# Which engine makes the low parts of tiles 10, 12, 16 and 18 of a split-precision mixture-of-experts kernel

## The reference

```python
x = x + 0.5 * ffn(layernorm(x), ...)      # B, T, D = 8, 512, 128
x = x + attn(layernorm(x), ...)           # two 128x128 projections, gates
x = x + 0.5 * ffn(layernorm(x), ...)

def ffn(x, centroids, expert_biases, Ws_up, Ws_down, W_up, W_down):   # E = F = 64, TOP_K = 8
    shared = silu(xf @ Ws_up) @ Ws_down
    aff = xf @ centroids.T
    _, idx = top_k(aff + expert_biases, TOP_K)
    w = sigmoid(take_along_axis(aff, idx))
    w = w / (sum(w) + 1e-08)
    cw = zeros((T, E)).at[arange(T)[:, None], idx].add(w)
    h = silu(einsum('td,edf->etf', xf, W_up))
    y = einsum('etf,efd->etd', h, W_down)
    return shared + einsum('etd,te->td', y, cw)
```

## Time and profile before

| what | value |
|---|---|
| median of 3 runs | 836.47 us (836.36 to 836.81) |
| profiled execution, span from first to last instruction | 834.9 us |
| PE / DVE / ACT / POOL busy | 809.7 / 698.6 / 654.2 / 404.6 us |
| granted PE clock | full (2.4 GHz level) in all slices |
| length of a body A phase / a body B phase | 50.3 / 51.6 us |

### The profile page before, as it was taken

How to read it: one execution, slowest core, us unless ns; L and a number is a source line. 1 busy time by engine, 2 the same in 40 slices (tenths; PEclk the granted TensorE clock), 3 DMA queues, 4 the chain that set the end, 5 groups by cost and what they waited for, 6 DMA issues and landing times.

```text
span 834.9 us, 12478 instructions
## 1 busy us (share of the span) xinstructions
PE 809.7 (97%) x3691; PEld 648.0 (78%) x3691; DVE 698.6 (84%) x1456; ACT 654.2 (78%) x1204; POOL 404.6 (48%) x355
## 2 busy tenths in 40 slices
PE   7899999999999999999999999999999999999998
PEld 5777778877778777787777877778778787788786
DVE  7998888798887988879888798787896987888875
ACT  5886679778787787877878788786878868876975
POOL 2764545544445444554545455354453644544443
PEclk9999999999999999999999999999999999999999
DMA  7000000000000000000000000000000000000000
GB/s 264 20 1 26 1 1 1 1 13 14 13 1 1 25 0 13 0 0 25 0 13 0 0 25 0 13 0 0 25 0 0 0 0 27 0 1 1 14 0 13
DMA packets 16046, 11.51 MB, mean 14 GB/s; under 512 B 1680, under 2 KB 14992, under 8 KB 16016
## 3 DMA queue, kind: packets, MB, share of 16 engines
q1 hardware_dynamic: 16016, 11.15, 4.2%
HBM read 9.05 MB, written 2.10 MB: 13 GB/s over the span
## 4 chain that ended last, share of the span: by engine, by line
PE 47%; DVE 18%; issue 15%; POOL 11%; ACT 7%; DMA 0%; POOLq 0%; DVEq 0%; ACTq 0%
POOL g_lo L351 8%; PE up L700 7%; PE up L701 7%; PE up L702 7%; PE y_ps L700 7%; PE y_ps L702 7%; PE y_ps L701 7%; DVE g_lo L578 3%; DVE up L569 3%; DVE gated L569 3%; DVE normed L515 2%; PE side L709 2%; ACT up L410 2%; ACT g_hi L418 2%; POOL rstd L341 2%
## 5 line engine op out<-in xcount | busy, mean ns | idle before, releaser
L351 POOL TENSOR_TENSOR g_lo<-gated,g_hi 128x512 fp32r<-128x512 f32 x256 | 332.3, 1298 | 370.9 <-ACT g_hi L418 370.3
L410 ACT ACTIVATE up<-up 128x512 f32<-128x512 f32 x528 | 310.9, 590 | 74.7 <-PE up L702 73.3
L569 DVE TENSOR_TENSOR gated<-up,cw 128x512 f32<-128x512 f32 x256 | 174.7, 682 | 51.6 <-ACT up L410 47.7
L569 DVE TENSOR_TENSOR up<-up,cw 128x512 f32<-128x512 f32 x256 | 175.9, 687 | 48.8 <-ACT up L410 45.5
L700 PE MATMUL up<-x_hi,wu_hi 128*128 128x512 f32 x512 | 204.3, 399 | 7.2 <-DVE g_lo L578 7.2
L700 PE MATMUL y_ps<-g_hi,wd_hi 128*128 128x512 f32 x512 | 208.4, 407 | 1.7 <-POOL g_lo L351 1.7
L702 PE MATMUL y_ps<-g_hi,wd_lo 128*128 128x512 f32 x512 | 202.4, 395 | 0.0
L701 PE MATMUL up<-x_lo,wu_hi 128*128 128x512 f32 x512 | 202.2, 395 | 0.0
L702 PE MATMUL up<-x_hi,wu_lo 128*128 128x512 f32 x512 | 201.9, 394 | 0.0
L701 PE MATMUL y_ps<-g_lo,wd_hi 128*128 128x512 f32 x512 | 201.8, 394 | 0.0
L418 ACT CAST g_hi<-gated 128x512 fp32r<-128x512 f32 x256 | 157.7, 616 | 48.1 <-DVE gated L569 45.8
(11 more groups left out here) (100 smaller groups left out, 564.1 us busy)
## 6 DMA issues: line engine op xcount, KB each, us to landing
x_in<-in_x SPq DMA_DIRECT2D x8, 256.0 KB, 2.7
wu_raw<-in_w_up SPq DMA_DIRECT2D x4, 512.0 KB, 5.8
wd_raw<-in_w_down SPq DMA_DIRECT2D x4, 512.0 KB, 6.8
x_res<-in_x SPq DMA_DIRECT2D x8, 256.0 KB, 2.7
out<-out_sb SPq DMA_DIRECT2D x7, 256.0 KB, 2.2
out<-out_sb SPq DMA_DIRECT2D x2, 128.0 KB, 1.8
sm_raw<-in_ident SPq DMA_DIRECT2D x2, 64.0 KB, 5.2
ident<-in_ident SPq DMA_DIRECT2D x1, 64.0 KB, 2.6
```

The costliest lines, as they stand in the source:

```text
L351: nc.gpsimd.tensor_tensor(g_lo[:, i, :], gated[:, t // 2 % ORING, :], g_hi[:, i, :].bitcast(fp32), ALU.subtract).then_inc(lo_done[1], 1)
L410: nc.scalar.activation(up[i][:, :], up[i][:, :], ACT.Silu).then_inc(silu_done, 1)
L569: nc.vector.tensor_tensor(gated[:, t // 2 % ORING, :] if t % 2 else up[i][:, :], up[i][:, :], cw[ph.q][:, :], ALU.mult).then_inc(gate_done, 1)
```

## The change

The split of the low parts between DVE and POOL by odd and even is replaced by two lists, `POOL_TILES` (the odd tiles and 10, 12, 16, 18) and `VECTOR_TILES` (the rest). `OWN[t]` says which list a tile is in, `RANK[t]` its place in it. All counts, buffers and waits that used `t % 2` and `t // 2` use them. For the four tiles the gate writes to `gated`, ACT's high part and POOL's low part read from there, and `free_bank` waits for the gate. The ring `gated` has five buffers in place of four. POOL has 20 low parts per phase (16 before), DVE 13 (17).

```diff
--- before.py
+++ after.py
@@ -17,8 +17,13 @@
 SLOTS = -(-NT // RING) * RING
 LAG = RING + 1
 GRING = LAG + 1
-ORING = 4
-NLOW = (NT // 2 + 1, NT // 2)
+
+POOL_TILES = sorted({t for t in range(NT) if t % 2} | {10, 12, 16, 18})
+VECTOR_TILES = [t for t in range(NT) if t not in POOL_TILES]
+OWN = [int(t in POOL_TILES) for t in range(NT)]
+RANK = [(VECTOR_TILES, POOL_TILES)[OWN[t]].index(t) for t in range(NT)]
+ORING = 5
+NLOW = (len(VECTOR_TILES), len(POOL_TILES))
 AW = D + 2
 AS = 256
 NPIECE = 4
@@ -239,7 +244,7 @@
         def low_count(ph, t):
 
             back, t = before(t)
-            return NLOW[t % 2] * (ph.p - back) + t // 2 + 1
+            return NLOW[OWN[t]] * (ph.p - back) + RANK[t] + 1
 
         def halves(ph, name, t):
 
@@ -348,7 +353,7 @@
 
                 i = t % GRING
                 pool.wait_ge(hi_done, NT * ph.p + t + 1)
-                nc.gpsimd.tensor_tensor(g_lo[:, i, :], gated[:, t // 2 % ORING, :], g_hi[:, i, :].bitcast(fp32),
+                nc.gpsimd.tensor_tensor(g_lo[:, i, :], gated[:, RANK[t] % ORING, :], g_hi[:, i, :].bitcast(fp32),
                                         ALU.subtract).then_inc(lo_done[1], 1)
 
             def split_up(i):
@@ -360,7 +365,7 @@
 
             def phase(ph):
                 for t in range(SLOTS):
-                    if (t - 1) % 2 and 0 < t <= NT:
+                    if 0 < t <= NT and OWN[t - 1]:
                         low_part(ph, t - 1)
                     if t in ph.at.get("wu_lo", ()):
                         split_up(ph.at["wu_lo"].index(t))
@@ -414,7 +419,7 @@
                     act.wait_ge(gate_done, NJ * ph.p + t)
                 else:
                     act.wait_ge(silu_done, NT * ph.p + t + 1)
-                src = gated[:, t // 2 % ORING, :] if t % 2 else up[t % RING][:, :]
+                src = gated[:, RANK[t] % ORING, :] if OWN[t] else up[t % RING][:, :]
                 nc.scalar.copy(g_hi[:, t % GRING, :], src).then_inc(hi_done, 1)
 
             def y_copy(p):
@@ -566,7 +571,7 @@
 
                 i = t % RING
                 dve.wait_ge(silu_done, NT * ph.p + t + 1)
-                nc.vector.tensor_tensor(gated[:, t // 2 % ORING, :] if t % 2 else up[i][:, :], up[i][:, :], cw[ph.q][:, :],
+                nc.vector.tensor_tensor(gated[:, RANK[t] % ORING, :] if OWN[t] else up[i][:, :], up[i][:, :], cw[ph.q][:, :],
                                         ALU.mult).then_inc(gate_done, 1)
 
             def low_part(ph, t):
@@ -601,7 +606,7 @@
                         dve.wait_ge(cw_done[ph.q], ph.use + 1)
                     if 0 < t < NT:
                         gate(ph, t)
-                    if t % 2 and 1 < t <= NT:
+                    if 1 < t <= NT and not OWN[t - 1]:
                         low_part(ph, t - 1)
                     if t in ph.at.get("wd_lo", ()):
                         split_low(wd_lo, wd_raw, wd_hi, ph.at["wd_lo"].index(t), wd_hi_done, wd_lo_done)
@@ -753,7 +758,7 @@
 
             def down_product(ph, t):
                 made, t = low_count(ph, t), before(t)[1]
-                pe.wait_ge(lo_done[t % 2], made)
+                pe.wait_ge(lo_done[OWN[t]], made)
                 i = t % GRING
                 if t > 0:
                     last = split_product(y_ps[:, :], (wd_hi[:, t - 1, :], wd_lo[:, t - 1, :]), (g_hi[:, i, :], g_lo[:, i, :]),
@@ -767,7 +772,7 @@
             def free_bank(ph, t):
 
                 back, tile = before(t)
-                if tile % 2:
+                if OWN[tile]:
                     pe.wait_ge(gate_done, NJ * (ph.p - back) + tile)
                 else:
                     pe.wait_ge(lo_done[0], low_count(ph, t))
```

## The result

The changed kernel takes 847.3 us (median of 4 runs, 847.12 to 847.64) against 836.57 of the kernel before beside it: a ratio of 1.0128, with a 95% interval of 1.0114 to 1.0143. The forecast was 848 us. The profiled execution has a span of 845.3 us, 10.4 more than before. Of all the executions timed for this document one, of `after_x2_psum`, ran at a lower granted clock (0.851) and took 883.8 us; it is left out.

The account below looks back on a forecast made before the run. PE, busy 97% of the span, was taken as the bound, so only holes in its matmul train count. 7.8 (body B, phase 2) + 1.2 (body A) + 2.4 (phases 1, 14) = 11.4 us, giving 848 us; range 833 to 853.

Parts of the forecast that it names:

- Holes removed: PE's idle gaps at tile 10 (body B) and tile 16 (body A) go: -0.66 us in each steady phase.
- Blocks queue behind POOL's operations: With POOL operations back to back, each normed block on DVE waits for one; body B's four take 5.1 us, before 1.4.
- Body B, +1.3: Five phases B and phase 2: new 1.95 us hole at PE's transpose of normed, one of 0.66 gone; 7.8 us in all.
- Body A, +0.2: Six phases: tile 17's down product waits for POOL, a hole of 0.85 us for one of 0.66; 1.2 us in all.
- Phases 1 and 14, +1.2 each: Four x2 blocks wait behind POOL's low parts; between -0.7 and +1.9 us each, taken as +1.2, 2.4 us in all.
- The sum: All phases together: 11.4 us more on the profiled execution, a span of 846.3 us.
- rival 1: The gain comes through, normed done before PE asks: -2.8 us, 833.7; chance 0.16.
- Rival 2: Low 17 waits for its high part, blocks three or four fall into that gap, body B about 0: 839 us; chance 0.20.
- rival 3: DVE blocks hold POOL in turn, down products wait too: +1 us in 12 phases, 857 to 860 us; chance 0.11.
- rival 4: Nothing moves, holes closed and opened cancel: 835 to 838 us; chance 0.07.

Follow-up runs that it names:

- after_x2_psum: The changed kernel with DVE's four x2 blocks in phases 1 and 14 reading their first operand from PSUM (wrong values): 843.23 us, 1.0076 of before.
- low_10: The changed kernel with only tile 10 added to POOL's odd tiles, not 12, 16 and 18: 833.89 us, 0.9970 of the kernel before.
- after_norm_psum: The changed kernel with DVE's normed blocks from x1 read from PSUM instead of SBUF (wrong values): 835.12 us, 0.9980 of the kernel before.
- u_t_later: The changed kernel with PE's transpose of normed and its copy two slots later in body B and phase 2: 847.46 us, 1.0131 of before.

## Why the prediction was right, step by step

- **Holes removed** (-0.66 in each steady phase). Right for both: neither the hole at tile 10 nor that at tile 16 is in the trace of after, and low_10 shows the 0.66 of body B alone, to the hundredth.
- **Blocks queue behind POOL's operations.** Right, and the main term. The pairs take 2.56 and 2.46 us; worked out were 2.5 and 2.5. after_norm_psum takes this one thing away, and the total falls below that of the kernel before. Two slips around it changed nothing in the sum: POOL is not "busy without a break", since the prediction's own clock has low 17 start 1.4 us after low 16 ends, as it does in the trace; and the four blocks took 1.57 us before, not 1.4, and 5.02 now, not 5.1.
- **Body B, +1.3.** Measured +1.39 each, phase 2 +1.44. The new hole is 1.96 us long (2.19 from the start of the matmul before it, less the pace of 0.23), as worked out. On phase 6's clock low 15 was put at 349.7 (it is 349.60), the end of the blocks at 356.3 (356.14), the transpose at 356.4 (356.29). Six of them were 7.8 us in the sum and are 8.4. What I said of the transpose as the place where PE waits is true, but u_t_later shows that it is not what the hole depends on.
- **Body A, +0.2.** The mechanism was right, the sign of the sum was not. The down product of tile 17 has its hole, of 1.06 us rather than 0.85: lows 15 and 16 take 2.74 us together, not 2.55. DVE's `biased`, which has both operands in SBUF, runs from 305.86 to 307.11, across the change from the one to the other; that it holds low 16 up is inferred from that. But I had only looked at the hole of tile 16, and two small ones of body A went as well: the transpose of `w_dup` at 318.55 and the first up product of the next phase at 322.71, some 0.3 and 0.2 us in the kernel before. So body A is 0.16 shorter, phase 13 0.63: -1.4 in the sum in place of +1.2.
- **Phases 1 and 14, +1.2 each.** They are +2.19 and +1.37, 3.6 us in place of 2.4. The term was mis-sized. It stood between bounds of -0.7 and +1.9, nearer the upper one, with no row for phase 14, and none for the 1.1 us of four unhindered `x2` blocks (after_x2_psum has them at 1.12). The `x2` blocks took 4.24 us (3.9 worked out), and after_x2_psum shows that they carry phase 14's loss and some two thirds of phase 1's. The rest of phase 1 is a cost that the prediction has nowhere: the 0.73 us of the down product of tile 11, which stands in the runs with tile 10 alone and with 10 and 12 as well. For phase 1 the upper bound that I gave, 1.9, was too low.
- **The sum** was 11.4 us on the span; 10.4 came. Body A was put 2.6 us too high, and phases 1, 2, 14 and body B 1.8 too low in all. That 847.3 lies so near to 848 is in part luck: the two errors have different causes, and most of the one is hidden by the other.
- **The rivals.** That the gain comes through (rival 1) was decided as named: block four ended after 354.4 by phase 6's clock of before, at 356.1. Rival 2 had the right pause, since low 17 does wait for its high part, but no block fell into it: gates and `w_sel` filled it. (Its 839 also is 1 to 2 us less than its own terms give, 836.5 with 1.2 for body A, 2.4 for phases 1 and 14, and up to 0.6 for body B.) That POOL falls behind because DVE holds it in turn (rival 3) is seen in small: the mean low part is 9 ns longer, 0.2 us at low 16 of body A. That nothing moves (rival 4) is out by the 10.7 us.

## What to carry to other kernels

Before work is moved to an engine with idle time, write down its queue over the slots where the work lands, and not its share of the whole run: POOL was idle half of the time, and eleven slots in which it had work for 15.2 of 15.4 us (the prediction's estimate) were enough. Look there for the operations of the neighbour that don't run beside it: the four moved low parts free DVE some 2.4 us per phase, and in body B they make four short blocks, 1.57 us before, take 5.02. Move single pieces to where one particular hole stands: tile 10 alone gave 0.3%, tiles 10 and 30 gave 0.45%, and 10, 12, 16 and 18 cost 1.3%.

## What the runs showed of the hardware

Some DVE operations that start while a POOL operation runs end up to 0.3 us after it, and several in a row wait for one POOL operation each when POOL has no gap. Here `normed` (a tensor_scalar from SBUF to SBUF), `x2`, `w_sel` and `biased` (two tensors in SBUF) did so. With their tensor, or one of the two, read from PSUM, the blocks of `normed` and `x2` took 0.73 us (two) and 1.12 us (four) beside a POOL that never stopped, at most 414 and 344 ns for one. A reduction from SBUF was not touched either: `w_sum` at 361.40 takes 0.40 us in the middle of `xu`. The Trainium skill (SBUF — State Buffer, "Who interferes with whom") says that the port pair is held for the whole instruction and the second one to come blocks; the runs agree. They add that with both queues full the two engines took turns instruction by instruction: two `normed` blocks took as long as lows 15 and 16 (2.56 and 2.54 us), so the row of short DVE operations went at the pace of POOL's long ones. A blocked DVE operation counts as busy in the profile, so the loss shows as longer DVE records and not as DVE's waits.

What I had not expected is how far from additive this is: halves of the change at -0.8 and +1.0 us, the whole at +10.7.
